# Waiting for one group of matmuls less before each gather in the last message-passing layer

## The chip, the cores and the metric

The kernel runs on one core of one Trainium2 chip, as one launch. The metric is the device time of that launch in microseconds (us). Five engines work side by side, each in the order of its own program, and they wait for each other by semaphores: PE (matrix multiply), DVE (vector), ACT (scalar, activation functions), POOL (GpSimd, which here builds the descriptors of gathers) and SP (which only starts transfers).

## The reference

A graph with 6250 nodes of 64 features and 206,250 edges (sorted by target node `dst`) goes through four layers. After each there is a residual sum and a layer norm. The change touches only the fourth layer, a message layer with a gated update:

```python
x = jnp.concatenate([node_features[src], node_features[dst], edge_features], axis=-1)
h = jax.nn.relu(x @ W1.T + b1)
messages = h @ W2.T + b2
agg = jax.ops.segment_sum(messages, dst, num_segments=n)
# then a GRU cell of agg and node_features
```

The kernel multiplies the node features by their parts of `W1` once per node (arrays `from_src_d` and `from_dst_d` in DRAM), so that an edge only needs one row of each, the product of its 32 edge features with the third part of `W1`, a sum and a relu. `W2` is applied after the sum over edges.

## The kernel before

The edges are cut into 51 blocks of 4096. In an earlier stage each block was laid out as a grid whose place gives the source node; what has no place in the grid goes to a short second list of 9 x 128 rows. `layer3_edges` takes one block after another. In block n the grid is worked off in seven groups of seven columns, numbered u = 0 to 6:

- PE, `turn_in(u)`: two transposes of edge features (L2556, L2557), which ACT copies back (`copies`, L2649, L2650).
- PE, `before_relu(n, u)`: 4 matmul records on edge features (L2566) and 21 on one-hot rows times target features (L2570) give the values before the relu. The last one adds one to the semaphore `pre_ready`.
- DVE, `add_src(n, u)` (L2711): waits for just that count of `pre_ready` and adds the source features. ACT and DVE then split the result in three bf16 parts.
- PE, `reduce(n, u)` (L2584, L2587): the sum over edges, three groups behind.

The second list is worked off beside it. Its rows can't be placed, so POOL gathers them by index: for each of the nine chunks c one indirect DMA from `from_src_d` (L2534) and one from `from_dst_d` (L2537), a pair per chunk, 18 gathers per block, into one of three buffers. DVE needs them all in `second_sum(n)` (L2745), after group 3 of block n. The DVE then goes on to `add_src(n, 4)`. After group 5, DVE turns the next block's 1.5 MB row table into a one-hot table (`mark`, L2750). The block ends with the window sums (L2800 to L2808).

What sets the order around the change is POOL's own program: it goes through the chunks in order, and ahead of chunks 0, 1, 3, 4, 6 and 7 it waits until PE has finished a certain group of `before_relu`. So the gathers of block n are spread over the time in which the other engines work on block n-1. `pre_ready` begins at 8, and after `before_relu(n, u)` it is 7n + u + 9. Before the change the waits are for these groups (number of the block, group):

```
chunk          0        1        3        4        6        7
before     n-1, 2   n-1, 3   n-1, 4   n-1, 5   n-1, 6   n, 0
```

Chunks 2, 5 and 8 follow at once. The loop bodies are unrolled 24 times, with the same order in each.

Of the kernel before, what the change touches and what calls it, by code (L numbers as in the profile page):

```python
# [675 lines left out]
def over_rounds(eng, z, k, body, turn=2):  # L676
    thirds = z.NBK // 3
    rounds = n_rounds(eng, k)
    with eng.Fori(0, rounds) as r:
        with eng.Fori(0, thirds // turn) as i:  # L680
            for h in range(turn):
                for j in range(3):
                    body(r * z.NBK + i * (3 * turn) + (h * 3 + j), r * thirds + i * turn + h, i * (3 * turn) + (h * 3 + j), j, r)
        for m in range(thirds - thirds % turn, thirds):
            for j in range(3):
                body(r * z.NBK + (m * 3 + j), r * thirds + m, m * 3 + j, j, r)
# [1748 lines left out]
def layer3_edges(nc, z, k, a):  # L2435
    NBK, NT = z.NBK, z.NT
    NS = NT // SUB
# [4 lines left out]
    with ExitStack() as ctx:  # L2442
# [42 lines left out]
        with nc.Block() as block:  # L2485
# [39 lines left out]
            @block.gpsimd  # L2525
            def _(pool):
                def body(n, m, b, j, r):
                    pool.wait_ge(row_in[j], m * 16 + 16)
                    pool.sem_inc(k.pool_steps, 1)
                    for c in range(SC):  # L2530
                        if c % 3 < 2:
                            pool.wait_ge(pre_ready, n * NS + (c // 3 * 2 + c % 3 + 4))
                            pool.sem_inc(k.pool_steps, 1)
                        pool.indirect_dma_start(ps_x[j][:, c, :], None, a["from_src_d"][:, :],  # L2534
                                                bass.IndirectOffsetOnAxis(ap=row[j][:, c, AT_SRC:AT_SRC + 1].bitcast(i32), axis=0)
                                                ).then_inc(x_in[j], 16)
                        pool.indirect_dma_start(qs_x[j][:, c, :], None, a["from_dst_d"][:, :],  # L2537
                                                bass.IndirectOffsetOnAxis(ap=row[j][:, c, AT_DST:AT_DST + 1].bitcast(i32), axis=0)
                                                ).then_inc(x_in[j], 16)

                over_rounds(pool, z, k, body, turn=8)
# [556 lines left out]
```

## Time and profile before

| | us |
|---|---|
| median of 3 runs | 8052.66 |
| lowest and highest run | 8046.71, 8058.54 |
| the profiled execution: its time | 8046.71 |
| its span from first to last instruction | 8045.1 |
| PE busy | 4979.4 (62%) |
| DVE busy | 4607.4 (57%) |
| POOL busy | 4401.4 (55%) |
| ACT busy | 1547.6 (19%) |
| gathers of the stage, x459 each, first to last start | 6288.6 to 7922.5 |

No engine is busy all the time, and the shares are means over stages that have different limits. The stage of the change lies between about 6290 and 7945 us, a fifth of the span. The times in a timeline are microseconds from the span's start. A row there gives the start of an instruction, its duration, engine and line, what it writes and reads, and in square brackets how long the engine stood idle before it and what ended that. "remote" there is a signal for which the profile names no instruction. The ends of PE's matmuls are worked out and not observed.

### The profile page before, as it was taken

The numbers are of one execution on the slowest core, as the hardware profiler recorded it, in microseconds if no ns is written. First come the engines' busy times: TensorE is split into PE (matmuls) and PEld (weight loads), VectorE is DVE, ScalarE is ACT, GpSimd is POOL, SyncE is SP. The second block draws the span as 40 slices with busy tenths as digits, with TensorE's granted clock in tenths as the row PEclk, the third lists the DMA queues.
The fourth block names the chain that finished last, engine by engine and source line by source line (L and its number), as shares of the span: only waits on it lengthen the run. The fifth ranks groups of instructions, "written<-read, shape, count | busy, mean of one in ns | idle before, by whom it ended". The sixth has DMA issues, their size and how long they took to land. (4 is left out here: it accounts for less than half of the span.)

```text
span 8045.1 us, 135870 instructions
## 1 busy us (share of the span) xinstructions
PE 4979.4 (62%) x47718; PEld 4204.6 (52%) x47719; DVE 4607.4 (57%) x8883; ACT 1547.6 (19%) x3166; POOL 4401.4 (55%) x4199
## 2 busy tenths in 40 slices
PE   2555545555455543323555556899998677777776
PEld 1333433333333332222455544899998566666665
DVE  4554545555555544444555555666666566666665
ACT  1111111111111110000111143000000344434442
POOL 3656556565656654554255555555553466656662
PEclk7666676767767666666567675999999899999998
DMA  3333333233333311112000031111111333333332
GB/s 127 120 111 114 118 107 127 101 125 111 115 114 111 127 46 37 29 29 25 11 23 22 23 110 33 27 25 26 27 26 27 123 111 102 105 101 107 109 102 56
DMA packets 303354, 621.11 MB, mean 77 GB/s; under 512 B 153436, under 2 KB 229902, under 8 KB 285521
## 3 DMA queue, kind: packets, MB, share of 16 engines
q1 hardware_dynamic: 153693, 405.75, 14.7%
q0 software_dynamic: 133216, 116.93, 6.5%
q10 hardware_dynamic: 15994, 92.31, 3.3%
q8 instruction: 297, 4.87, 0.3%
q14 instruction: 154, 1.26, 0.1%
HBM read 547.78 MB, written 235.06 MB: 97 GB/s over the span
## 5 line engine op out<-in xcount | busy, mean ns | idle before, releaser
L349 POOL DMA_INDIRECT pay_d<-row,place x1632 | 1733.0, 1062 | 1216.2 <-issue 544.0
L462 PE MATMUL win<-onehot,val 128*128 128x128 f32 x4998 | 858.6, 339 | 270.1 <-issue 161.9
L462 PEld LDWEIGHTS win<-onehot,val 128*128 128x128 f32 x4998 | 779.1, 244 | 467.6 <-issue 282.3
L2032 PE MATMUL g_win<-g_hot,y_part 128*128 128x128 bf16 x14994 | 867.4, 219 | 21.7 <-issue 12.0
L2012 POOL DMA_INDIRECT g_x<-xg_d,g_row x459 | 580.1, 1264 | 538.4 <-PE g_win L2032 411.3
L2032 PEld LDWEIGHTS g_win<-g_hot,y_part 128*128 128x128 bf16 x14994 | 845.6, 98 | 35.1 <-issue 18.0
L2534 POOL DMA_INDIRECT m_from_src<-from_src_d,m_row x459 | 539.1, 1174 | 523.1 <-PE m_pre L2570 206.4
L565 DVE TENSOR_TENSOR hot<-near_dve,drel 128x896 bf16<-128x896 bf16 x357 | 222.6, 624 | 936.8 <-remote 698.8
L716 POOL DMA_INDIRECT lo_row_and_x<-in_x,r_row x459 | 438.0, 954 | 418.7 <-PEq L839 232.8
L1275 POOL DMA_INDIRECT sorted_d<-s_row,s_place x459 | 441.0, 961 | 323.5 <-DVE s_place L1391 138.3
L832 PE MATMUL r_win<-r_onehot,r_val 128*128 128x160 f32 x918 | 211.8, 409 | 556.2 <-DVEq L856 543.5
L2537 POOL DMA_INDIRECT m_from_dst<-from_dst_d,m_row x459 | 476.6, 1038 | 139.9 <-issue 137.8
L432 PE MATMUL pair<-hot_hi,hot_lo 128*128 128x392 bf16 (+3 forms) x1632 | 293.0, 345 | 406.3 <-DVE hot_hi L503 347.5
L832 PEld LDWEIGHTS r_win<-r_onehot,r_val 128*128 128x128 f32 x918 | 197.0, 277 | 580.5 <-DVEq L856 558.9
L443 PE MATMUL pair<-upto,lo_hot 128*128 128x49 bf16 x1632 | 97.0, 202 | 630.7 <-ACT upto L382 470.6
L432 PEld LDWEIGHTS pair<-hot_hi,hot_lo 128*128 128x128 bf16 x1632 | 199.0, 128 | 525.2 <-issue 231.2
L2566 PE MATMUL m_pre<-m_w_four,m_ea_t 96*128 96x192 f32 (+1 forms) x1428 | 450.7, 397 | 20.2 <-issue 19.8
L2711 DVE TENSOR_TENSOR m_hid<-m_pre,p_nodes 128x448 f32<-128x448 f32 x357 | 221.6, 621 | 417.8 <-remote 295.4
L370 ACT ACTIVATE onehot<-hot 128x896 f32<-128x896 bf16 x357 | 334.5, 952 | 580.1 <-DVE hot L565 556.7
L2081 DVE TENSOR_TENSOR g_hot<-iota,g_drel 128x896 bf16<-128x896 f32 x364 | 374.5, 1087 | 110.7 <-PE g_win L2032 102.4
L443 PEld LDWEIGHTS pair<-upto,lo_hot 128*128 128x128 bf16 x1632 | 72.6, 108 | 649.9 <-issue 649.0
L2570 PEld LDWEIGHTS m_pre<-m_q_win,m_hot_t 128*128 128x128 bf16 x7497 | 337.7, 101 | 131.5 <-issue 62.9
(455 smaller groups left out, 11027.1 us busy)
## 6 DMA issues: line engine op xcount, KB each, us to landing
m_hot_t<-drow_d SPq DMA_DIRECT2D x52, 1568.0 KB
scan_d<-in_none ACTq DMA_DIRECT2D x51, 1034.2 KB
lo_row_and_x<-lo_d SPq DMA_DIRECT2D x51, 1024.0 KB
m_grid<-pay_d SPq DMA_DIRECT2D x52, 882.0 KB
pay_d<-in_fill SPq DMA_DIRECT2D x51, 882.0 KB
grid<-pay_d SPq DMA_DIRECT2D x51, 882.0 KB
pay_d<-in_fill SPq DMA_DIRECT2D x51, 648.0 KB
sorted_d<-in_none ACTq DMA_DIRECT2D x51, 581.8 KB
```

What stands on the lines that cost most here:

```text
L349: pool.indirect_dma_start(a["pay_d"][:, :], bass.IndirectOffsetOnAxis(ap=place[j][:, c:c + 1], axis=0), row[j][:, c, :], None).then_inc(ro ...
L432: last = mm(pair[h][:, q, c * NT:BK * NT].rearrange("p (n s) -> p n s", s=NT), hot_lo[:, e, :], hot_hi[:, e, 0:NT].unsqueeze(1).to_broadca ...
L462: last = mm(win[:, :], val[u % 2][:, s, :], onehot[u % 2][:, s, :], start=(u == 0 and s == 0), stop=(u == NS - 1 and s == SUB - 1))
L716: pool.indirect_dma_start(k.xs[j][:, c, :], None, a["x"][:, :], bass.IndirectOffsetOnAxis(ap=k.row[j][:, c, AT_SRC:AT_SRC + 1].bitcast(i32 ...
L832: mm(win[j][:, :], val[j][:, c, :], onehot[j][:, c, :], start=(c == 0), stop=(c == SC - 1))
L1275: pool.indirect_dma_start(a["sorted_d"][:, :], bass.IndirectOffsetOnAxis(ap=place[j][:, c:c + 1], axis=0), row[j][:, c, :], None).then_inc ...
L2012: pool.indirect_dma_start(xs[j][:, c, :], None, a["xg_d"][:, :], bass.IndirectOffsetOnAxis(ap=row[j][:, c, AT_SRC:AT_SRC + 1].bitcast(i32) ...
L2032: last = mm(win[:, h, 0:W], k.y[q][:, t, h * P:(h + 1) * P], hot[u][:, s, :], start=(t == 0 and q == 0), stop=(t == NT - 1 and q == 2))
L2081: v.tensor_tensor(hot[u][:, :, :], k.iota[:, :].unsqueeze(1).to_broadcast([P, SUB, W]), twos(drel[j][:, u * SUB:(u + 1) * SUB])[:, :, 0:1] ...
L2534: pool.indirect_dma_start(ps_x[j][:, c, :], None, a["from_src_d"][:, :], bass.IndirectOffsetOnAxis(ap=row[j][:, c, AT_SRC:AT_SRC + 1].bitc ...
L2537: pool.indirect_dma_start(qs_x[j][:, c, :], None, a["from_dst_d"][:, :], bass.IndirectOffsetOnAxis(ap=row[j][:, c, AT_DST:AT_DST + 1].bitc ...
L2566: mm(out[:, first * D:(first + size) * D], ea_t[u % 2][0:size * F, o:o + P], w_four[0:size * F, 0:size * D], start=True, stop=False)
```

## The change

In POOL's program the number that each of the six waits asks for is one lower. All else is the same: no engine's instructions are added, removed or moved.

```diff
                         if c % 3 < 2:
-                            pool.wait_ge(pre_ready, n * NS + (c // 3 * 2 + c % 3 + 4))
+                            pool.wait_ge(pre_ready, n * NS + (c // 3 * 2 + c % 3 + 3))
                             pool.sem_inc(k.pool_steps, 1)
```

The waits are now for these groups:

```
chunk          0        1        3        4        6        7
after      n-1, 1   n-1, 2   n-1, 3   n-1, 4   n-1, 5   n-1, 6
```

## Rows read from the trace of the kernel before

**Rows 1.** The page's costliest groups: the stage's first gather.

```profile
L2534 POOL DMA_INDIRECT m_from_src<-from_src_d,m_row x459 | 539.1, 1174 | 523.1 <-PE m_pre L2570 206.4
```

**Rows 2.** The line of second_sum: count, durations, first and last start.

```profile
L2745 DVE TENSOR_TENSOR m_from_src<-m_from_src,m_from_dst x51: 745/748/807, 6319.7 to 7930.1; 128x576 f32<-128x576 f32 x51
```

**Rows 3.** Waits in 6300 to 7920 us: total, times, longest.

```profile
DVE m_hid L2711 <- remote: 294.3, 130, 15.1
...
DVE m_hid L2711 <- PE m_pre L2570: 92.6, 55, 9.2
```

**Rows 4.** POOL in one block: start, duration, instruction, idle time before it.

```profile
6755.72 0.94 POOL L2534 DMA_INDIRECT m_from_src<-from_src_d,m_row  x1 [3.73 <-PE m_pre L2570]
...
6759.47 1.02 POOL L2537 DMA_INDIRECT m_from_dst<-from_dst_d,m_row  x1 [0.30 <-issue]
6762.38 1.23 POOL L2534 DMA_INDIRECT m_from_src<-from_src_d,m_row  x1 [1.89 <-remote]
...
6769.08 0.95 POOL L2537 DMA_INDIRECT m_from_dst<-from_dst_d,m_row  x1 [0.30 <-issue]
6771.84 1.23 POOL L2534 DMA_INDIRECT m_from_src<-from_src_d,m_row  x1 [1.81 <-remote]
...
6777.32 2.12 POOL L2534 DMA_INDIRECT m_from_src<-from_src_d,m_row  x1 [0.30 <-issue]
...
6782.95 0.95 POOL L2537 DMA_INDIRECT m_from_dst<-from_dst_d,m_row  x1 [0.30 <-issue]
6787.64 0.95 POOL L2534 DMA_INDIRECT m_from_src<-from_src_d,m_row  x1 [3.75 <-PE m_pre L2570]
```

**Rows 5.** DVE in the same block, same columns.

```profile
6755.70 0.62 DVE L2711 TENSOR_TENSOR m_hid<-m_pre,p_nodes 128x448 f32<-128x448 f32 x1 [1.32 <-PE m_pre L2570]
...
6758.51 0.62 DVE L2711 TENSOR_TENSOR m_hid<-m_pre,p_nodes 128x448 f32<-128x448 f32 x1 [1.66 <-remote]
...
6761.63 0.62 DVE L2711 TENSOR_TENSOR m_hid<-m_pre,p_nodes 128x448 f32<-128x448 f32 x1 [0.38 <-remote]
...
6765.90 0.75 DVE L2745 TENSOR_TENSOR m_from_src<-m_from_src,m_from_dst 128x576 f32<-128x576 f32 x1
6771.09 0.62 DVE L2711 TENSOR_TENSOR m_hid<-m_pre,p_nodes 128x448 f32<-128x448 f32 x1 [4.44 <-remote]
...
6776.65 1.98 DVE L2750 TENSOR_SCALAR m_hot_t<-m_hot_t,iota_p 128x6272 bf16<-128x6272 bf16 x1
...
6786.00 0.29 DVE L2808 TENSOR_TENSOR acc<-m_win,acc 128x128 f32 x1 [0.39 <-issue]
6787.62 0.62 DVE L2711 TENSOR_TENSOR m_hid<-m_pre,p_nodes 128x448 f32<-128x448 f32 x1 [1.33 <-PE m_pre L2570]
```

**Rows 6.** PE in the same block: the ends of before_relu 1 and 4.

```profile
6756.21 0.43 PE L2570 MATMUL m_pre<-m_q_win,m_hot_t 128*128 128x64 bf16 x9
...
6765.61 0.43 PE L2570 MATMUL m_pre<-m_q_win,m_hot_t 128*128 128x64 bf16 x9
```

**Rows 7.** POOL in the last block, where no later block's gathers exist.

```profile
7923.70 0.95 POOL L2537 DMA_INDIRECT m_from_dst<-from_dst_d,m_row  x1 [0.30 <-issue]
```

**Rows 8.** DVE in the last block.

```profile
7930.10 0.75 DVE L2745 TENSOR_TENSOR m_from_src<-m_from_src,m_from_dst 128x576 f32<-128x576 f32 x1
7930.76 0.62 DVE L2711 TENSOR_TENSOR m_hid<-m_pre,p_nodes 128x448 f32<-128x448 f32 x1
```

**Rows 9.** POOL where one block of other rhythm hands over to the next.

```profile
7755.48 0.95 POOL L2537 DMA_INDIRECT m_from_dst<-from_dst_d,m_row  x1 [0.30 <-issue]
```

**Rows 10.** DVE in that block and at the hand-over.

```profile
7728.02 0.62 DVE L2711 TENSOR_TENSOR m_hid<-m_pre,p_nodes 128x448 f32<-128x448 f32 x1 [1.34 <-issue]
...
7740.00 0.62 DVE L2711 TENSOR_TENSOR m_hid<-m_pre,p_nodes 128x448 f32<-128x448 f32 x1
...
7754.79 0.29 DVE L2808 TENSOR_TENSOR acc<-m_win,acc 128x128 f32 x1 [0.40 <-issue]
7757.67 0.62 DVE L2711 TENSOR_TENSOR m_hid<-m_pre,p_nodes 128x448 f32<-128x448 f32 x1 [2.59 <-PE m_pre L2570]
```

## The prediction, made before the changed kernel ran

> **What bounds the kernel now.** I began with the page's list of the costliest groups, to see where POOL's gathers stand: 459 gathers from `from_src_d` at 1174 ns in the mean, with about as much idle time of POOL before them as work [rows 1]. POOL isn't full, so it doesn't bound the stage by its work. Next I asked whether anybody waits for what the gathers bring. The only taker is `second_sum`. All 51 of them take 745 to 807 ns [rows 2], and in the block that I read closely the one at 6765.90 has no idle time before it [rows 5]. So gathers that come sooner relieve no wait for their data.
>
> Then the waits of the stage, summed. DVE stands idle for 294.3 us in 130 waits before `add_src`, ended by "remote", and for 92.6 us ended by PE [rows 3]. `add_src` waits only for `pre_ready`. That is the wait to explain, so I put three timelines of one ordinary block side by side. It runs from the `add_src` of group 0 at 6755.70 to the next block's at 6787.62, 31.92 us [rows 5].
>
> POOL's 18 gathers come in three series there [rows 4]. I call them A, B and C:
> - A: 2 pairs, 6755.72 to 6759.47 + 1.02 = 6760.49 (chunks 7 and 8), started by group 0.
> - B: 3 pairs, 6762.38 to 6769.08 + 0.95 = 6770.03 (chunks 0, 1, 2), started by group 2.
> - C: 4 pairs, 6771.84 to 6782.95 + 0.95 = 6783.90 (chunks 3 to 6), started by group 4.
>
> Inside a series a gather follows the one before after 0.30 us. The waits of chunks 1, 4 and 6 are met when they are reached.
>
> Now DVE [rows 5] beside PE [rows 6]. The matmuls of `before_relu` 4 end at 6765.61 + 0.43 = 6766.04, yet `add_src` of group 4 starts at 6771.09, 5.05 us later, and DVE has nothing to do for 4.44 us of it. It starts 1.06 us after series B ends, and POOL, which waits for the same group, 0.75 us after DVE. Group 2: `add_src` starts at 6761.63, 1.14 us after series A ends. Group 1 ends on PE at 6756.64 and DVE starts at 6758.51, in the middle of series A. I read this as follows: PE's signal isn't seen while POOL issues gathers back to back, and comes about 1.1 us after a series has ended. The last block speaks for it. There no later block's gathers exist, POOL's last one ends at 7924.65 [rows 7], and `add_src` of group 4 starts at 7930.76, right behind `second_sum` at 7930.10, without idle time [rows 8].
>
> So a block is as long as the way from group 0 to group 4's signal, and after it DVE works nearly without a gap to the block's end: 6787.62 - 6771.09 = 16.53 us. The change acts on where the three series lie.
>
> **The change part by part.** Every wait asks for one group less. What that does to the series:
> - Series C starts with group 4's signal as before, but its first chunk is now 4, since chunk 3 went with group 3. It takes chunks 4 to 8, five pairs. The wait of chunk 7 (now group 6 of the same block) is met when it is reached.
> - Series A is now chunk 0 alone, one pair, started by group 1.
> - Series B is chunks 1, 2, 3, again three pairs, again started by group 2.
>
> *Series A and the start of series B.* Before, group 2's signal came 1.14 us after two pairs that began at 6755.72. Now one pair begins 0.75 us after group 1's `add_src`. At best that is released with PE's end at 6756.64: the pair then runs from 6757.4 to 6759.6 (1.25 us apart, the last 0.95), and `add_src` of group 2 starts 1.14 us later, at 6760.7, 0.9 us sooner than 6761.63. At worst the tail of series C holds PE back. C's five pairs end 2 x 1.25 = 2.50 us after the four did, at 6786.40. One block earlier that is 6754.48, plus 1.06 is 6755.54. PE then needs another 1.6 us for group 1, so `add_src` comes at 6757.2, the pair ends at 6760.2, and group 2 is released at 6761.3, 0.3 us sooner. I take 0.3 us, because the hold is what the rows show at every series' end.
>
> *Series B to group 4.* Three pairs as before, triggered by the same group, with DVE and ACT doing the same work behind that group. The distance 6771.09 - 6761.63 = 9.46 us stays. I price this part at nothing. The cover is that the pattern is the same; if it is lost, the rivals below hold.
>
> *The seam between blocks.* The two gathers that series C gains run where POOL was idle before, from about 6784.2 to 6786.40. DVE's last instruction of the block starts at 6786.00 and the next `add_src` at 6787.62 [rows 5]; 6786.40 + 1.06 is 6787.46, just before it. So the signal of group 0 need not be late. There is one hand-over in the trace that looks like this: a gather ends at 7755.48 + 0.95 = 7756.43 [rows 9], and `add_src` follows at 7757.67, 1.24 us after it, 2.88 us after L2808 instead of 1.62 [rows 10]. By that distance the seam here would end at 6787.64. Price: nothing, with up to 1.5 us as the other end (second rival).
>
> *DVE's port.* One gather takes 2.12 us at 6777.32 while DVE runs `mark` (1.98 us from 6776.65) [rows 4, 5]; this stays inside series C.
>
> The Trainium skill ("SBUF — State Buffer", on who interferes with whom) says that only VectorE and GpSimd share a port pair, by an exclusive lock, and that TensorE has its own. The 2.12 us agree. By that rule alone gathers would not hold back PE's signal at all, group 4 would be late for another reason, and the change would be worth nothing (first rival); the last block of this trace speaks against that.
>
> *Once, at the start.* The first block's gathers have nothing to wait for up to chunk 6, now up to chunk 8: four more gathers in the opening series, 5 us at most; the series they would have made later is saved. I count +3 us.
>
> The sum: 0.3 us x 50 blocks = -15 us, +3 us, together -12 us. On the profiled execution's own time that is 8046.7 - 12 = 8035. It lay 6 us below the median of the three runs, so I say 8041 against 8052.66. The gain's bounds are 0.9 x 50 = 45 us and nothing.
>
> **The rivals.**
> 1. *Nothing changes.* POOL and group 4 have a common cause that I don't see, or 0.3 us is eaten up by slower gathers. For it: the pattern is so stable that the same waits can fall into place. Against it: the last block. Time: 8053.
> 2. *Slower: the seam closes.* L2808 waits for PE's last `reduce`. If the tail of series C holds that signal as series B holds group 4, L2808 starts at 6786.40 + 1.06 = 6787.46 and not at 6786.00, 1.46 us later, and the next block with it. 50 x 1.46 = 73 us: 8126. It decides as soon as the last `reduce` or the first transposes of a block get their signal out only behind POOL's last gather. For it: the 2.88 us in rows 10, where POOL was still at work. Against it: there L2808 itself had only 0.40 us of idle time before it although POOL was gathering around it, so DVE's own work seems to let signals through.
> 3. *Much faster: group 4 slips through.* In one block the `add_src` of group 4 starts 11.98 us after that of group 0 (7740.00 and 7728.02) and not 15.39, while POOL gathers all the time, and the block takes 29.65 us [rows 10]. If the shifted series makes this the rule, up to 2.27 us x 50 = 114 us go: 7939; if for half the blocks, 7996. For it: the signal misses its chance by little, as PE's matmuls end only a little after DVE's string of work begins. Against it: series B keeps its place against group 2, and such blocks are few.
>
> **How the numbers follow.** Forecast 0.45, nothing changes 0.17, seam 0.25, slipping through 0.13. About 0.2%, 16 us, is what a measurement of this kernel can tell from no change. Of the forecast's 0.45 (its own range 8008 to 8056) some 0.25 is beyond 16 us, 0.20 within. Faster is 0.25 + 0.13 = 0.38, same is 0.20 + 0.17 = 0.37, slower is 0.25. The range runs from 7975, which takes in a good part of rival 3, to 8125, where rival 2 is half through.
>
> **What would show it.** Right: POOL's series are 1, 3 and 5 pairs, the one before group 2's `add_src` ends about half a microsecond sooner, DVE's idle time before group 4's `add_src` is still about 4.4 us, and L2808 to the next `add_src` is still about 1.6 us. Wrong: idle time before L2808 or in front of the block's first transposes (rival 2), a block's idle time before group 4 gone (rival 3), or 31.9 us per block unchanged with the series moved (rival 1). If group 5's or 6's `add_src` is the one that now waits, the pattern has broken up and none of my sums holds.

## The result, and the profile after

| | before | after |
|---|---|---|
| median of 3 runs, us | 8052.66 | 8141.47 |
| lowest and highest run | 8046.71, 8058.54 | 8135.45, 8153.40 |
| the profiled execution | 8046.71 | 8125.93 |
| PE busy, us | 4979.4 | 5066.6 |
| DVE busy, us | 4607.4 | 4609.9 |
| POOL busy, us | 4401.4 | 4420.1 |

The change made the kernel slower: after over before is 1.0127, with 1.0107 to 1.0146 as its 95% interval. I had forecast 8041 us and a range up to 8125; the time lies 16 us beyond it, on the other side of 8052.66. The profiled execution of the kernel after is the fastest of the 29 on record (8125.93 to 8180.25 us), so what is read from it rather understates the loss.

All of it arises in the stage of the change. From `add_src`'s first start to the one that opens the last block are 1611.5 us before and 1697.2 us after, 85.7 us more (the profiled executions differ by 79.2). DVE and POOL don't work more: their busy times are the same to 19 us. So for them it is waiting, and the sum of waits says for whom. PE's busy time did grow, by 87.2 us with the same instructions; I come back to that below. The waits of the stage after, from 6300 to 8010 us (engine, what it was about to do, what ended the idle time; total us, times, longest):

```profile
POOL m_from_src L2534 <- PE m_pre L2570: 380.4, 115, 15.2
...
DVE m_hid L2711 <- remote: 206.7, 57, 16.4
...
DVE m_hid L2711 <- PE m_pre L2570: 162.4, 144, 9.3
...
PE m_pre L2570 <- issue: 123.6, 191, 1.2
...
DVE m_hot L2706 <- remote: 100.7, 41, 5.5
...
DVE m_hot L2706 <- PE m_win L2584: 35.1, 33, 1.6
```

Against [rows 3], `add_src` itself waits no longer than before: 206.7 + 162.4 = 369.1 us against 294.3 + 92.6 = 386.9. But DVE now also waits 100.7 + 35.1 us ahead of L2706, the one-hot rows for `reduce`, which waits for PE too. The stalls have moved to other places of the block. POOL's wait for PE ahead of L2534 rose from 206.4 us [rows 1] to 380.4. The PE line tells something else: PE itself stood idle in the middle of `before_relu`, where its program waits for nothing ("issue" is idle time for which the profile shows no signal that was waited for). Before the change that line reads 34.4 us in 57 times.

Where the stalls are is seen in the starts of `add_src`, averaged over the 50 blocks behind the first and counted from group 0's (worked out from the starts of L2711, 7 per block):

| group | 1 | 2 | 3 | 4 | 5 | 6 | next 0 |
|---|---|---|---|---|---|---|---|
| before, us | 2.98 | 6.02 | 8.23 | 15.08 | 18.63 | 22.66 | 32.23 |
| after, us | 1.71 | 4.64 | 9.39 | 14.46 | 19.94 | 24.13 | 33.95 |

Groups 1 and 2 come sooner, as forecast, even by more (1.38 us at group 2). Then 0.76 us are lost on the way from 2 to 4, 1.93 us from 4 to 5, and 0.41 us to the block's end. That is 1.72 us per block, 86 us in 50.

Now one block of the kind that is commonest in this trace. POOL after, answering to [rows 4] (start, duration, instruction, idle time before it):

```profile
6909.70 1.22 POOL L2534 DMA_INDIRECT m_from_src<-from_src_d,m_row  x1 [3.62 <-PE m_pre L2570]
...
6912.54 1.22 POOL L2534 DMA_INDIRECT m_from_src<-from_src_d,m_row  x1 [0.37 <-issue]
...
6919.29 0.95 POOL L2537 DMA_INDIRECT m_from_dst<-from_dst_d,m_row  x1 [0.30 <-issue]
6922.43 1.11 POOL L2534 DMA_INDIRECT m_from_src<-from_src_d,m_row  x1 [2.19 <-PE m_pre L2570]
```

DVE in that block, answering to [rows 5]:

```profile
6907.31 0.62 DVE L2711 TENSOR_TENSOR m_hid<-m_pre,p_nodes 128x448 f32<-128x448 f32 x1 [1.33 <-PE m_pre L2570]
...
6911.80 0.62 DVE L2711 TENSOR_TENSOR m_hid<-m_pre,p_nodes 128x448 f32<-128x448 f32 x1 [0.21 <-PE m_pre L2570]
...
6917.01 0.62 DVE L2711 TENSOR_TENSOR m_hid<-m_pre,p_nodes 128x448 f32<-128x448 f32 x1 [2.99 <-remote]
...
6921.43 0.62 DVE L2706 TENSOR_TENSOR m_hot<-m_near_dve,m_drel 128x896 bf16<-128x896 bf16 x1 [2.73 <-remote]
...
6922.64 0.62 DVE L2711 TENSOR_TENSOR m_hid<-m_pre,p_nodes 128x448 f32<-128x448 f32 x1
...
6939.63 0.29 DVE L2808 TENSOR_TENSOR acc<-m_win,acc 128x128 f32 x1 [0.40 <-issue]
6942.81 0.62 DVE L2711 TENSOR_TENSOR m_hid<-m_pre,p_nodes 128x448 f32<-128x448 f32 x1 [2.89 <-PE m_pre L2570]
```

Chunk 0's pair goes out at 6909.70, behind group 1. Group 2's `add_src` starts at 6911.80, while that pair is still being issued (to about 6912.2). So POOL finds the wait of chunk 1 met when it gets there: 0.37 us instead of a pause, and chunks 0 to 3 become one series of 4 pairs, 6909.70 to 6920.24. Inside it group 3 is held (6917.01), and then PE's signal that L2706 needs, until 6921.43, 1.19 us after the series. The block takes 35.50 us, of which 3.18 lie between L2808 and the next `add_src`.

What PE did meanwhile shows that more than a signal is held. PE in that block, in `before_relu` 4 and behind it:

```profile
6919.86 0.28 PE L2570 MATMUL m_pre<-m_q_win,m_hot_t 128*128 128x64 bf16 x4 [1.07 <-issue]
6921.27 0.37 PE L2570 MATMUL m_pre<-m_q_win,m_hot_t 128*128 128x64 bf16 x4 [1.14 <-issue]
6921.48 2.66 PE L2612 MATMUL m_pre_s<-m_w_four,m_ea_s 128*128 128x256 f32 x6
```

And PE in the block of [rows 6], before group 4's `add_src` at 6771.09:

```profile
6765.88 1.47 PE L2612 MATMUL m_pre_s<-m_w_four,m_ea_s 128*128 128x256 f32 x6
...
6768.30 0.28 PE L2556 MATMUL m_ea_ps<-ident,m_ea 128*128 128x128 f32 x1
```

Before the change PE had finished group 4 and had gone on to the second list's matmuls (L2612), one `reduce` and the next transposes while DVE still waited for group 4. The times of the semaphore updates, which the trace also keeps, agree: the signals of these four pieces of work came at 6771.06, 6771.14, 6771.28 and 6771.32, within 0.26 us, although their last matmuls end at 6766.04, 6767.35, 6768.46 and 6768.69. Work that takes PE 2.65 us can't be done in 0.26 us, so the signals were late and not the work. In the stage before, the first two of the four lie under 0.2 us apart in 47 of 50 blocks; with the gathers left out (below) they lie 1.31 us apart in all 50, as the matmuls' ends do.

After the change the long series begins earlier, and PE comes to a halt sooner. Group 4's own matmuls go out in pieces, from 6915.48 to 6921.64, with idle time of up to 1.14 us between them. From the first to the last of them are 4.40 us in the mean of the stage, against 1.62 before. What PE used to do during the wait for group 4, it now does behind it, so group 5 comes late even when its own signal isn't held. That is where the 1.93 us go in this block: group 5's `add_src` starts 5.62 us after group 4's. The granted clock plays in as well. It was 1.00 in all of the block of [rows 5]. Here it was 0.50 in 6923 to 6927 us (1.2 GHz, the lower of the two levels), after PE had been busy for only 2.14 of 4 us in 6915 to 6919 and for 2.00 in 6919 to 6923; L2612 took 2.66 us instead of 1.47. Over the stage the granted clock was 0.96 before and 0.90 after, and PE's busy time there rose from 1277.4 to 1369.9 us. How much of the loss is the clock's own is not separated by any run. Within the series 2, 3, 4 of the kernel before it made no difference (32.04 us in 21 blocks at full clock, 32.05 in the 21 others).

And one block that is as I forecast it, with 1, 3 and 5 pairs. POOL:

```profile
6878.45 0.95 POOL L2534 DMA_INDIRECT m_from_src<-from_src_d,m_row  x1 [5.46 <-PE m_pre L2570]
...
6882.08 1.23 POOL L2534 DMA_INDIRECT m_from_src<-from_src_d,m_row  x1 [1.43 <-PE m_pre L2570]
```

DVE:

```profile
6881.33 0.62 DVE L2711 TENSOR_TENSOR m_hid<-m_pre,p_nodes 128x448 f32<-128x448 f32 x1 [0.29 <-PE m_pre L2570]
...
6883.47 0.62 DVE L2711 TENSOR_TENSOR m_hid<-m_pre,p_nodes 128x448 f32<-128x448 f32 x1
...
6890.77 0.62 DVE L2711 TENSOR_TENSOR m_hid<-m_pre,p_nodes 128x448 f32<-128x448 f32 x1 [4.42 <-remote]
```

Here group 2 comes after the pair, POOL pauses 1.43 us, group 3 comes in that pause without idle time, and only group 4 is held, for 4.42 us. Over the stage, such blocks took 30.65 us in the mean, but there are 8 of them. The series by number of pairs, counted from POOL's starts in 49 blocks (all but the first and the last), with the mean length of those blocks:

| kernel | series (pairs) | blocks | mean us |
|---|---|---|---|
| before | 2, 3, 4 | 42 | 32.05 |
| after | 4, 2, 3 | 20 | 34.63 |
| after | 1, 3, 5 | 8 | 30.65 |
| after | 3, 6 | 8 | 33.63 |
| after | 3, 3, 1, 2 | 5 | 34.10 |
| after | 1, 5, 1, 2 | 5 | 36.62 |
| after, second trace | 1, 3, 5 | 21 | 31.92 |
| after, second trace | 4, 2, 3 | 14 | 35.37 |
| after, second trace | 1, 3, 2, 3 | 7 | 36.09 |
| after, second trace | 1, 5, 1, 2 | 6 | 36.34 |

The second trace is that of the same changed kernel, run again in batch 2 below. The mixture isn't fixed: there the pattern that I forecast is the commonest. It is shorter than the kernel before's in the first trace and the same within 0.13 us in the second. In both it is the other patterns that lose the time; what failed is that the pattern stays.

### The profile page after: what moved, and what is told of

It reads as the page before. It is cut to its first block and busy times, and to the rows that moved or that the text cites. A ratio compares the mean times of both kernels' runs of the same rounds, so it can differ in the third digit from the quotient of the medians.

```text
span 8124.3 us, 135870 instructions
## 1 busy us (share of the span) xinstructions
PE 5066.6 (62%) x47718; PEld 4254.5 (52%) x47719; DVE 4609.9 (57%) x8883; ACT 1551.5 (19%) x3166; POOL 4420.1 (54%) x4199
## 5 line engine op out<-in xcount | busy, mean ns | idle before, releaser
L2534 POOL DMA_INDIRECT m_from_src<-from_src_d,m_row x459 | 519.6, 1132 | 584.6 <-PE m_pre L2570 380.4
L2537 POOL DMA_INDIRECT m_from_dst<-from_dst_d,m_row x459 | 514.6, 1121 | 139.9 <-issue 132.3
L2570 PEld LDWEIGHTS m_pre<-m_q_win,m_hot_t 128*128 128x128 bf16 x7497 | 354.2, 102 | 244.4 <-issue 176.2
L2570 PE MATMUL m_pre<-m_q_win,m_hot_t 128*128 128x64 bf16 x7497 | 395.0, 199 | 128.9 <-issue 127.9
L2711 DVE TENSOR_TENSOR m_hid<-m_pre,p_nodes 128x448 f32<-128x448 f32 x357 | 222.1, 622 | 377.9 <-remote 206.7
```

The costliest lines, as they stand in the source:

```text
L2570: last = mm(out[:, s * D:(s + 1) * D], hot_t[j][:, (u * SUB + s) * P:(u * SUB + s + 1) * P], q_win[j][:, q * D:(q + 1) * D], start=False, ...
```

## The experiments

My theory: POOL's gathers, issued one behind the other, hold back PE's signals, and a block's length is set by where POOL pauses. The rivals: the gathers have nothing to do with group 4, or it is their data that hurt. In the code that was tried, the condition and the sum are replaced by a table, where an entry v asks for group v - 2 of block n - 1, and 9 and 10 for groups 0 and 1 of block n:

```diff
-                        if c % 3 < 2:
-                            pool.wait_ge(pre_ready, n * NS + (c // 3 * 2 + c % 3 + 4))
+                        asks = {...}
+                        if c in asks:
+                            pool.wait_ge(pre_ready, n * NS + asks[c])
```

The table that equals the kernel before is `{0: 4, 1: 5, 3: 6, 4: 7, 6: 8, 7: 9}`; of the changed kernel `{0: 3, 1: 4, 3: 5, 4: 6, 6: 7, 7: 8}`. The kernels below with a table have one line more, so `add_src` is L2712 there and the last window sum L2809.

The runs came in five batches. In two of them (the first and the fourth) the kernel before itself took 6647.15 and 6652.39 us, and in the three others 8076.19, 8023.27 and 8035.89. Each kernel is compared only with the kernel before of its own batch. I call the two the short and the long regime.

### Batch 1, short regime: is it the gathers, and which edit

**All gathers left out** (their buffers are zeroed once, so the second list's terms are missing from the result):

```diff
-                        pool.indirect_dma_start(ps_x[j][:, c, :], None, a["from_src_d"][:, :],
...
-                        pool.indirect_dma_start(qs_x[j][:, c, :], None, a["from_dst_d"][:, :],
...
-                    dve.wait_ge(x_in[j], m * (2 * SC * 16) + 2 * SC * 16)
```

> Leaves out all 918 gathers of the stage (the second list's features are zeros), POOL keeps its waits. Hold theory (PE's signal isn't seen while POOL issues gathers in a row): the add of group 4 comes about 10 to 12 us after that of group 0 and not 15, a block takes 25 to 27 us and not 32, the whole 7740 to 7820. Data theory (the gathers' transfers disturb PE): the same. Seam theory (only what POOL does at the block's end costs): nothing against before, since POOL is idle there before: 8050.

**The same bytes brought by plain loads on SP's queue**, 128 rows at fixed places instead of the rows asked for:

```diff
+                        sp.dma_start(ps_x[j][:, c, :], a["from_src_d"][c * P:(c + 1) * P, :]).then_inc(x_in[j], 16)
+                        sp.dma_start(qs_x[j][:, c, :], a["from_dst_d"][c * P:(c + 1) * P, :]).then_inc(x_in[j], 16)
```

> The 18 transfers of a block are plain loads of 128 rows each, started by SP, to the same buffers; POOL issues nothing. The rows are not the ones of the index. Hold theory: as without gathers, 7740 to 7850, since POOL's issuing is what holds the signal. Data theory: as long as before, 8000 to 8150.

**Only chunk 7's wait earlier**, `7: 8`, all else as before:

> Waits as before, but chunk 7 waits for group 6 of the block before, as in the changed kernel. Seam theory: all of the loss is here, 8120 to 8160. Hold theory: the series after group 0 goes, groups 1 and 2 are seen at once, but the first series now starts on group 2 and falls on group 3; 8000 to 8100.

**All but chunk 7's**, `{0: 3, 1: 4, 3: 5, 4: 6, 6: 7, 7: 9}`:

> The changed waits for chunks 0, 1, 3, 4 and 6, chunk 7 waits as before for group 0 of its own block. Seam theory: no loss, 8050. Hold theory: chunks 7, 8 and 0 become one series of three pairs from group 0 on, group 2 is held until about 10 us after the block's start instead of 8: 8130 to 8220.

Measured: 6629.44 us, ratio 0.9971 (0.9960 to 0.9982); 6634.15, 0.9980 (0.9969 to 0.9990); 6649.21, 1.0005 (0.9995 to 1.0014); 6650.26, 1.0003 (0.9993 to 1.0013). Every expectation of a large effect missed: in this regime hardly anything is held, and the waits matter little. DVE in one block with only chunk 7's wait earlier:

```profile
5498.26 0.62 DVE L2712 TENSOR_TENSOR m_hid<-m_pre,p_nodes 128x448 f32<-128x448 f32 x1 [1.33 <-issue]
...
5506.87 0.62 DVE L2712 TENSOR_TENSOR m_hid<-m_pre,p_nodes 128x448 f32<-128x448 f32 x1
...
5523.40 0.62 DVE L2712 TENSOR_TENSOR m_hid<-m_pre,p_nodes 128x448 f32<-128x448 f32 x1 [1.32 <-PE m_pre L2571]
```

Group 4 comes 8.61 us after group 0, not 15.39 as in [rows 5], without idle time, and the block takes 25.14 us. Yet POOL gathers all the while:

```profile
5498.20 0.94 POOL L2535 DMA_INDIRECT m_from_src<-from_src_d,m_row  x1 [0.30 <-issue]
...
5523.74 0.94 POOL L2535 DMA_INDIRECT m_from_src<-from_src_d,m_row  x1 [0.30 <-issue]
```

Of the stage's 918 gathers only 3 start behind a pause of over 0.6 us. In 342 groups of that trace the last matmul ends inside such a series, and the semaphore's update follows 0.01 us later in the median and never more than 0.5 us. So a gather doesn't hold PE's signal everywhere and always. The batch told nothing of the result, which belongs to the long regime, and so the kernels were run again.

### Batch 2, long regime: the cause and its size

**The changed kernel again**, same edit:

> The changed kernel itself, beside the kernel before on the same chip. On the first chip before took 8053 us and this 8141. In the first four experiments before took 6647 on another chip and a block of the stage 25.7 us, with hardly a wait for PE's signal. Hold theory (there PE's signal is held behind POOL's gathers and here it isn't): where before takes 6650, the change makes no difference, 6640 to 6660; where it takes 8050, 8120 to 8160. Seam theory (the two gathers that now lie over the block's end cost the time by themselves): 1% slower on either chip, 6710 where before is 6650.

8139.50 us, 1.0074 (1.0050 to 1.0098): slower again, by less than in the first measurement, since the kernel before took 8076.19 here.

**All gathers left out**, the edit of batch 1:

> Leaves out all gathers of the stage. Hold theory: where before takes 8050, 7740 to 7820; where it takes 6650, 6625 to 6635 as in the first run. Data theory: the same.

7689.97 us, 0.9519 (0.9495 to 0.9542). A block now takes 25.4 us. DVE in one:

```profile
6774.36 0.62 DVE L2707 TENSOR_TENSOR m_hid<-m_pre,p_nodes 128x448 f32<-128x448 f32 x1 [1.32 <-PE m_pre L2564]
...
6782.92 0.61 DVE L2707 TENSOR_TENSOR m_hid<-m_pre,p_nodes 128x448 f32<-128x448 f32 x1
...
6799.88 0.62 DVE L2707 TENSOR_TENSOR m_hid<-m_pre,p_nodes 128x448 f32<-128x448 f32 x1 [1.34 <-issue]
```

Group 4 at 8.56 us after group 0, and no idle time. That the gathers cause group 4's stall is shown here, and "nothing changes" through a common cause falls. The time is 50 us below the expectation. Their price in the kernel before is 8076.19 - 7689.97 = 386 us. The granted clock of the stage is 0.996 without them, against 0.958 in the kernel before, so a part of this price may be the clock's.

**Only chunk 7's wait earlier**:

> Hold theory: where before takes 8050, between 8000 and 8100; where 6650, no difference. Seam theory: where before takes 8050, 8120 to 8160.

8196.53 us, 1.0146 (1.0119 to 1.0172), above what either theory expected. Here the seam does close: from L2809 to the next `add_src` are 6.07 us in the mean, and in the block below L2809 itself waits.

```profile
6762.10 0.29 DVE L2809 TENSOR_TENSOR acc<-m_win,acc 128x128 f32 x1 [3.72 <-remote]
6766.11 0.62 DVE L2712 TENSOR_TENSOR m_hid<-m_pre,p_nodes 128x448 f32<-128x448 f32 x1 [3.72 <-PE m_pre L2571]
```

POOL's series are then 1 and 8 pairs in 19 blocks. So my second rival is a real mechanism, but not the main one in the changed kernel: there that distance is 2.13 us in the mean, against 1.95 before (2.35 in its second trace).

**No waits at all**:

```diff
-                        if c % 3 < 2:
-                            pool.wait_ge(pre_ready, n * NS + (c // 3 * 2 + c % 3 + 4))
-                            pool.sem_inc(k.pool_steps, 1)
```

> POOL's six waits for groups of matmuls are gone; its 18 gathers of a block run in a row as soon as the rows are there and the buffer is free, two blocks ahead. Hold theory: where before takes 8050, one series of 22.5 us per block at an arbitrary place and signals held in it, 8100 to 8500; where before takes 6650, no difference, 6640 to 6660.

8687.93 us, 1.0754 (1.0727 to 1.0781), worse than expected; 44.96 us for a block with one series of 9 pairs, 48 of the 49 counted. The 18 gathers of such a series end at 6850.69 + 0.94 = 6851.63. POOL:

```profile
6829.48 0.94 POOL L2531 DMA_INDIRECT m_from_src<-from_src_d,m_row  x1 [24.47 <-DMA m_row<-pay_d]
...
6850.69 0.94 POOL L2534 DMA_INDIRECT m_from_dst<-from_dst_d,m_row  x1 [0.30 <-issue]
```

DVE:

```profile
6828.96 0.61 DVE L2708 TENSOR_TENSOR m_hid<-m_pre,p_nodes 128x448 f32<-128x448 f32 x1
...
6835.24 0.62 DVE L2708 TENSOR_TENSOR m_hid<-m_pre,p_nodes 128x448 f32<-128x448 f32 x1 [3.38 <-remote]
...
6855.33 0.62 DVE L2708 TENSOR_TENSOR m_hid<-m_pre,p_nodes 128x448 f32<-128x448 f32 x1 [5.64 <-remote]
```

Groups 0 to 3 come before the series. Group 4 comes inside it, group 5 only behind it, 20.09 us after group 4. The waits are what keeps POOL from running on; each one that is already met when POOL comes to it is a pause lost.

### Batch 3, long regime: which pauses

**Series of 2, 2 and 5 pairs**, `{0: 2, 2: 4, 4: 6}`:

> Three waits per block: chunk 0 for group 0 of the block before, chunk 2 for group 2, chunk 4 for group 4. So series of 2, 2 and 5 pairs, where before has 2, 3 and 4. Hold theory: the series in front of group 4 is one pair (2.5 us) shorter, so group 4's add comes 2 to 2.5 us sooner, and the seam costs up to 0.5 us: where before takes 8060, 7950 to 7990; on a chip where before takes 6650, no difference. Seam theory (what lies over the block's end costs the time): slower than before, 8130.

8110.74 us, 1.0107 (1.0090 to 1.0124). Slower, where I had expected 7950 to 7990. Half of the reasoning came true: group 4 starts 12.72 us after group 0 in the mean, 2.4 sooner than before, and blocks with that pattern can be short (40 blocks, from 28.8 to 37.9 us, mean 31.91). Here the clock, or what goes with it, does make a difference: 29.53 us in the 9 of them at full clock, 32.60 in the 31 others. But 9 blocks take 39.96 us. In them only one gather of chunk 2's pair goes out (at 7496.90 in the block below) and then, after 1.43 us, 13 more without a pause. POOL, first and last of the 13:

```profile
7499.56 1.23 POOL L2538 DMA_INDIRECT m_from_dst<-from_dst_d,m_row  x1 [1.43 <-issue]
...
7515.25 0.94 POOL L2538 DMA_INDIRECT m_from_dst<-from_dst_d,m_row  x1 [0.31 <-issue]
```

DVE:

```profile
7502.42 0.62 DVE L2712 TENSOR_TENSOR m_hid<-m_pre,p_nodes 128x448 f32<-128x448 f32 x1 [1.24 <-PE m_pre L2571]
...
7516.82 0.62 DVE L2712 TENSOR_TENSOR m_hid<-m_pre,p_nodes 128x448 f32<-128x448 f32 x1 [9.10 <-remote]
```

Group 4 slips through at 7502.42, the wait of chunk 4 is met at once, and group 5 is held to 7516.82, 14.40 us later. This is the changed kernel's fault in a plainer form: a signal that gets through early costs the pause that the next one needs.

**One group later**, `{0: 5, 1: 6, 3: 7, 4: 8, 6: 9, 7: 10}`:

> Each of the six waits asks for one group more than before, the change in the other direction. Hold theory: chunk 6 waits for group 0 and chunk 7 for group 1 of the own block, series start on groups 0, 1, 3 and 5, and the series on group 3 holds group 4: 8020 to 8200 where before takes 8060. Theory that sooner is worse by itself: below 8060.

8099.46 us, 1.0097 (1.0077 to 1.0118); 33.55 us per block. The other direction is as bad, so the kernel before stands in a dip between two worse tables.

**All but chunk 7's**:

> Waits of the changed kernel, but chunk 7 as before on group 0 of its own block. Hold theory: chunks 7, 8 and 0 make one series of three pairs in front of group 2, held until 10 us after the block's start: 8130 to 8220 where before takes 8060. Seam theory: no loss.

8200.76 us, 1.0224 (1.0203 to 1.0244). Mostly 3, 3 and 3 pairs (38 blocks, 34.64 us): group 2 comes at 8.5 us and group 4 at 17.5. The wait before `add_src` from 6300 to 8010 us (total us, times, longest):

```profile
DVE m_hid L2712 <- remote: 409.0, 139, 5.0
```

With the edit of chunk 7 alone this makes two parts that each cost more than the whole (1.0146 and 1.0224, while both together cost 1.0127 or 1.0074). The parts don't add up, since each one moves the series against the groups anew.

**The same bytes by SP's loads**:

> The 18 transfers of a block are plain loads of 128 rows started by SP; POOL issues none. Not the rows of the index. Hold theory: as without gathers, 7680 to 7740 where before takes 8060. Data theory: about 8060.

7678.07 us, 0.9572 (0.9553 to 0.9591), 25.42 us per block, and `add_src` waits little, and for no signal of unknown origin. The largest row of its waits:

```profile
DVE m_hid L2708 <- PE m_pre L2567: 67.7, 89, 7.4
```

As many bytes come and go without harm, so it isn't their amount that holds PE's signal. It is something in the gathers that POOL issues. This run changes three things at once, the engine that issues, the queue and the rows read, and so it doesn't tell POOL's issuing from the transfers of its queue. One thing speaks for the issuing: in the kernel before, group 2's held signal came 1.09 us behind POOL's last gather in the median of 46 blocks, and 0.61 us before the last packet of that gather had ended.

### Batches 4 and 5: a better table

What was left open after batch 3: whether the harm is the five pairs at the block's end or the series that run together in front. Three tables, run first in a batch that turned out to be of the short regime, then again.

**Chunk 0 one group sooner than in the changed kernel**, `{0: 2, 1: 4, 3: 5, 4: 6, 6: 7, 7: 8}`, which differs from it in one number and keeps the five pairs:

> The changed kernel with one number other: chunk 0 waits for group 0 instead of group 1. Merging theory (in the changed kernel group 2's signal often comes before chunk 0's pair is out, so POOL doesn't pause, chunks 0 to 3 become one series from 2.4 us on, and groups 3 and 5 are held): the pair ends before group 2's signal, the pause is back, series of 1, 3 and 5 pairs in nearly every block, group 4's add at 14 to 15 us, a block 30.5 to 31.5 us: 7970 to 8020 where before takes 8050. Theory that five pairs at the end are what costs: as the changed kernel, 8120 to 8150.

> As chunk_0_after_group_0, which ran where before took 6652 and PE's signals were not held. Where before takes about 8050, merging theory: series of 1, 3 and 5 pairs in nearly every block, a block 30.5 to 31.5 us, 7970 to 8020. Theory that five pairs at the end cost: 8120 to 8150. Where before takes 6650 again: no difference.

**2, 2, 5 with the waits between kept**, `{0: 2, 2: 4, 3: 5, 4: 6, 6: 7, 7: 8}`:

> Series of 2, 2 and 5 pairs as in two_two_five, with waits on groups 3, 5 and 6 in front of chunks 3, 6 and 7, which only bite when a series would run on. Merging theory: the blocks of 37 to 40 us (every third to fifth there, in which 13 gathers ran on or group 6 was held to 28) shorten to 34, the others stay at 29.7 to 32; mean 30.8 instead of 33.4, 7980 to 8020 where before takes 8050. Theory that five pairs at the end are what costs: slower than before, 8110.

> As two_two_five_guarded. Where before takes about 8050, merging theory: 7980 to 8020. Theory that five pairs at the end cost: 8110. Where before takes 6650: no difference.

**A pause bought with group 3**, `{0: 3, 1: 5, 3: 5, 4: 6, 6: 7, 7: 8}`, the changed kernel with chunk 1 asking for group 3:

> The changed kernel, but chunk 1 waits for group 3 instead of group 2 and so pauses POOL in every block. Merging theory: group 3's add at 6 to 7 us in every block instead of 9.4, series of three pairs from 7.5 to 15, group 4 at 16, a block 32 to 33 us: about 8050 to 8100, less than the changed kernel although POOL starts later. Theory that five pairs at the end are what costs: 8140 or more.

> As pause_by_group_3. Where before takes about 8050, merging theory: 8050 to 8100. Theory that five pairs at the end cost: 8140 or more. Where before takes 6650: no difference.

In the short regime all three stand by the kernel before: 6645.74 (0.9989, 0.9980 to 0.9998), 6648.36 (0.9991, 0.9982 to 1.0000) and 6649.27 (0.9990, 0.9980 to 1.0000).

In the long regime they part.

*Chunk 0 after group 0*: 8021.17 us, 0.9983 (0.9968 to 0.9999), where the changed kernel had 1.0127 and 1.0074. One number undoes the whole loss. POOL in a block of 1, 3 and 5 pairs:

```profile
6757.04 0.94 POOL L2535 DMA_INDIRECT m_from_src<-from_src_d,m_row  x1 [1.92 <-PE m_pre L2571]
...
6760.73 1.24 POOL L2535 DMA_INDIRECT m_from_src<-from_src_d,m_row  x1 [1.40 <-PE m_pre L2571]
```

DVE:

```profile
6756.29 0.62 DVE L2712 TENSOR_TENSOR m_hid<-m_pre,p_nodes 128x448 f32<-128x448 f32 x1 [2.54 <-PE m_pre L2571]
...
6769.52 0.62 DVE L2712 TENSOR_TENSOR m_hid<-m_pre,p_nodes 128x448 f32<-128x448 f32 x1 [2.38 <-remote]
...
6784.44 0.29 DVE L2809 TENSOR_TENSOR acc<-m_win,acc 128x128 f32 x1 [0.39 <-issue]
6786.05 0.62 DVE L2712 TENSOR_TENSOR m_hid<-m_pre,p_nodes 128x448 f32<-128x448 f32 x1 [1.31 <-PE m_pre L2571]
```

Chunk 0's pair is out by 6759.32, before group 2 comes, so POOL pauses 1.40 us ahead of chunk 1. Group 4 then starts 13.23 us after group 0, and the block takes 29.76 us, with five pairs at its end and no loss at the seam. The rest of the expectation missed, by little in the time and clearly in the pattern: 1, 3, 5 holds in only 15 blocks (31.0 us), 1, 2, 6 in 26 (31.16). POOL pauses behind chunk 0 in all 49. Over all blocks the seam takes 2.90 us, 0.95 more than in the kernel before, so what lies over the block's end isn't free; the groups before it come sooner by more than that. The granted clock of the stage is back at 0.949. So five pairs at the end alone don't explain the changed kernel's loss; what differs is the pause ahead of chunk 1.

*2, 2, 5 guarded*: 8037.31 us, 1.0004 (0.9993 to 1.0015). The long blocks are cut from 40 to 34 us (9 blocks with series of 4, 1, 7 and 6 gathers), but the time is the kernel before's, above what I expected of it.

*Pause by group 3*: 8176.32 us in two runs, 1.0178 (1.0149 to 1.0207), a miss. The pause is there, but group 4's signal now slips through, the wait of chunk 4 is met, five pairs run on and group 5 is the one that is late (its matmuls take 5.67 us from first to last in the mean). DVE:

```profile
6745.89 0.62 DVE L2712 TENSOR_TENSOR m_hid<-m_pre,p_nodes 128x448 f32<-128x448 f32 x1 [1.33 <-PE m_pre L2571]
...
6758.10 0.62 DVE L2712 TENSOR_TENSOR m_hid<-m_pre,p_nodes 128x448 f32<-128x448 f32 x1 [2.67 <-remote]
...
6767.07 0.62 DVE L2712 TENSOR_TENSOR m_hid<-m_pre,p_nodes 128x448 f32<-128x448 f32 x1 [0.20 <-remote]
```

Group 4 at 12.21 us, group 5 at 21.18, and the block takes 35.00. So "restore the pause before chunk 1" was too narrow a rule. The wider one fits this kernel, the changed one and 2, 2, 5: whichever group gets through early makes POOL run on, and the next group pays. It isn't a law either. In the 26 blocks of 1, 2, 6 pairs in the kernel *chunk 0 after group 0*, group 4 gets through inside the last series at 13.04 us, POOL runs on with six pairs, and group 5 follows 3.41 us later, unheld. What is paid there is paid at the seam (3.28 us).

## Why the prediction was wrong

- *What bounds the kernel.* Right in the main. The gathers' data relieve no wait, and POOL's gathers hold back PE's signals: without gathers the block falls from 32 to 25.4 us, with the same bytes by SP to 25.42. What I didn't see is that PE's own matmuls halt too when a series lasts (123.6 us of idle time ahead of L2570 after, 34.4 before).
- *Series A and the start of series B.* Right in direction, wrong in its reason. I took it that chunk 0's pair holds group 2 as two pairs had, and that group 2 would come 1.14 us after it. It comes before the pair has ended in the block shown (6911.80), on the average 4.64 us after group 0 (5.21 in the second trace), when my best case was 5.0. [Rows 5] had the warning: group 1's `add_src` at 6758.51 is in the middle of series A. I noted it and drew nothing from it.
- *Series B to group 4.* This is the step that failed: "The distance 6771.09 - 6761.63 = 9.46 us stays. I price this part at nothing." It stays only if POOL pauses before series B, and POOL pauses only if group 2 hasn't come by the end of chunk 0's pair. A cover "that the pattern is the same" was no cover, since the step before it moved the one thing that makes the pattern. Measured: +0.76 us from group 2 to 4. The larger part was lost in a second term that I also left as it was, the 16.53 us from group 4 to the block's end: +1.93 us from group 4 to 5 and +0.41 behind it. That stretch is short only when PE has got its later work out before group 4's signal comes, and in the longer series PE halts before it has. Together this is +3.10 us per block, against 1.38 gained at group 2, where I had 0.3 gained and nothing lost. A chunk 0 that is released one group sooner brings the pause back and takes the loss away.
- *The seam.* Nearly right: 2.13 us in the mean against 1.95, 9 of the 86 us. The rival that I gave 0.25 has its mechanism elsewhere, and its 8126 us, close to the time measured, is a coincidence.
- *Once at the start.* Too small to be seen beside 85.7 us.
- *What would show it.* My last sentence there was the right test: "If group 5's or 6's `add_src` is the one that now waits, the pattern has broken up and none of my sums holds." It should have been a rival with a price. It could have been worked out from the rows: four pairs in one series are 4 x 2.50 = 10.0 us, and groups 3 and 4 are due inside it.
- The chances. That the pattern is so stable (42 of 49 blocks), I took as a sign that it would survive. My reading now, which no run tests by itself, is that it was stable because each series ended before the next group could get through, and the change takes just that away.

The Trainium skill ("SBUF — State Buffer", the section "Who interferes with whom") gives TensorE a port of its own. The plain loads agree as far as data go, since they held nothing, and in the short regime hardly anything is held. But in the long regime leaving out POOL's gathers gives 386 us back and PE's signal comes 6.5 us sooner at group 4, so a free port isn't a free signal.

The Trainium skill ("Perfetto Trace Analysis", the section "Tensor Engine Instruction (MATMUL, LD_WEIGHTS)") says that a matmul's end in the profile is estimated from the instruction's size. So that end alone can't say whether the 5.05 us between it and `add_src` are a late signal or slow work of PE. The four signals within 0.26 us, shown with the result, can: in that block the signal was late.

What stays open: what makes the two regimes, which signal gets through inside a series (group 4 in the kernel without waits does, group 5 doesn't), why PE's matmuls halt in a long one, and how much of the loss is the granted clock's. *Chunk 0 after group 0* is the best of the tables, by little: 8021.17 against 8035.89 of its batch, a ratio whose interval (0.9968 to 0.9999) just leaves out 1, and 0.9989 (0.9980 to 0.9998) in the short regime.

## What to carry to other kernels

Waits that throttle an engine are worth as much as the pause that they make, and a wait that is already met when the engine gets there makes none. When such waits are moved, work out for each one whether it still stops the engine, in time order, before any distance in the pattern is taken as kept. And try each part alone with care: here two parts each cost more than the whole, and one number of six decided between a loss of 1% and none.

## What the runs showed of the hardware

- Gathers that POOL issues back to back (0.95 us each, 0.30 us between) held PE's signals in the long regime: 15.39 us from group 0 to 4 in [rows 5] against 8.56 without them. The held signals then came out together: four within 0.26 us, for work that had ended over 2.65 us. Plain loads of the same size on SP's queue held nothing.
- In a long series PE's matmuls halt as well: group 4's take 4.40 us from first to last in the mean of the changed kernel's blocks, 1.62 in the kernel before and 1.62 without gathers. The granted clock of the stage is 0.90, 0.96 and 1.00 in these three.
- The same program has two regimes, 6650 and 8050 us. One chip showed both, in batches 1 and 3 (6647.15 and 8023.27). In the short one another stage waits less too, with the same busy time. POOL's longest gather loop, with only chunk 7's wait earlier, in the short regime (busy, mean ns, then idle time before):

```profile
L349 POOL DMA_INDIRECT pay_d<-row,place x1632 | 1714.4, 1051 | 588.7 <-issue 571.9
```

and the same kernel in the long one:

```profile
L349 POOL DMA_INDIRECT pay_d<-row,place x1632 | 1728.4, 1059 | 1155.5 <-issue 532.6
```

  The busy times agree to 1% and the idle time is doubled. The mean granted clock of PE was 0.822 and 0.763. What sets the regime was not found; a comparison across batches would have been worthless here, 1400 us apart, and only a kernel before run in the same batch made the verdicts possible.
